# A state-space stage rebuilt: convolution folded into the projection, and the last norm of the mixture moved into it

## The reference

```python
xz = x @ W_in + b_in                       # 128 -> 512
x_main, gate = xz[..., :256], xz[..., 256:]
x_main = silu(causal_conv(x_main, conv_w, taps=3, per channel) + conv_b)
dt = sigmoid(x_main @ W_dt + b_dt); Bm = x_main @ W_B + b_B; Cm = x_main @ W_C + b_C
state = (1 - dt) * state + dt * Bm;  y = Cm * state        # a scan over the 1024 tokens
y = (y - mean(y)) * rsqrt(var(y) + 1e-5)                   # over the 64 states
y = y @ W_si + b_si + D * x_main
y = y * sigmoid(gate)
out = y @ W_out + b_out
```

## Time and profile before

| | |
|---|---|
| median of 3 runs | 829.82 us (828.91 to 830.15) |
| profiled execution | 827.14 us, span of the trace 825.4 us |
| TensorE busy | 740.8 us, 90% of the span |
| VectorE, ScalarE, GpSimd busy | 462.3, 390.0, 439.0 us |
| mean granted TensorE clock | 0.956 of full |
| first mixture, from its first load to its last addition | 501 to 637 us |
| state space, first projection to the second mixture's first matmul | 643.0 to 703.0 us |

### The profile page before, as it was taken

One profiled execution on the slowest core, in us unless ns is written; L12 is line 12 of the kernel. 1 busy time (PEld: TensorE's weight loads), 2 busy tenths in 40 slices (PEclk: granted clock), 3 DMA queues, 4 the chain that ended last, 5 costly groups with the idle time before them and its releaser, 6 DMA issues. The chain is left out here.

```text
span 825.4 us, 14251 instructions
## 1 busy us (share of the span) xinstructions
PE 740.8 (90%) x5448; PEld 495.9 (60%) x5448; DVE 462.3 (56%) x1232; ACT 390.0 (47%) x483; POOL 439.0 (53%) x316
## 2 busy tenths in 40 slices
PE   2789999999999999999999989988998856679998
PEld 2456555655555565556556547867887522657787
DVE  5765565666556556655755501555455774655343
ACT  2345556555555555555555441355444740255422
POOL 4356775676667658656855680044343553144343
PEclk9699999999999999999999999999999885899999
DMA  2000000000000000000000006132231000033232
GB/s 64 8 1 1 9 1 1 8 1 2 8 1 2 7 2 1 8 2 1 2 1 26 2 1 147 27 120 87 66 104 39 0 1 0 0 106 113 67 106 77
DMA packets 29459, 25.15 MB, mean 30 GB/s; under 512 B 10128, under 2 KB 20944, under 8 KB 29392
## 3 DMA queue, kind: packets, MB, share of 16 engines
q1 hardware_dynamic: 29392, 24.25, 10.1%
HBM read 22.92 MB, written 1.31 MB: 29 GB/s over the span
## 5 line engine op out<-in xcount | busy, mean ns | idle before, releaser
L378 POOL TENSOR_TENSOR all_x<-all_x,at_probs 128x1024 f32<-128x1024 f32 (+3 forms) x128 | 222.9, 1741 | 35.7 <-ACT at_probs L453 21.0
L453 ACT ACTIVATE at_probs<-at_ring 128x1024 f32<-128x1024 f32 x144 | 147.3, 1024 | 113.8 <-PE at_ring L625 107.3
L498 DVE CUSTOM_DVE_ANT_0 at_ring<-at_ring,at_after_query 128x128 f32<-128x128 f32 (+3 forms) x256 | 119.5, 521 | 74.1 <-PE at_ring L590 74.1
L643 PE MATMUL at_out<-at_probs,at_k_nat 128*64 128x512 f32 (+3 forms) x768 | 140.3, 494 | 1.1 <-DVE a_attn_t L521 0.9
L1079 POOL TENSOR_TENSOR m_prod<-m_gate,m_wb 128x512 f32<-128x512 f32 x64 | 81.8, 1283 | 110.6 <-ACT m_gate L936 85.5
L378 POOL TENSOR_TENSOR all_x<-at_probs 128x768 f32<-128x768 f32 (+1 forms) x32 | 66.9, 2091 | 126.5 <-ACT at_probs L453 126.3
L990 DVE TENSOR_TENSOR m_hid<-m_prod,m_u 128x512 f32<-128x512 f32 x64 | 44.0, 687 | 88.7 <-POOL m_prod L1079 84.4
L643 PEld LDWEIGHTS at_out<-at_probs,at_k_nat 128*64 128x64 f32 x768 | 49.2, 136 | 69.9 <-issue 66.0
L494 DVE TENSOR_REDUCE at_half_max<-at_ring 128x2 f32<-128x1024 f32 x64 | 75.5, 1222 | 12.4 <-PE at_ring L590 12.4
L936 ACT ACTIVATE m_gate<-m_g 128x512 f32<-128x512 f32 x72 | 42.9, 599 | 82.2 <-PE m_g L847 81.7
L855 PEld LDWEIGHTS m_acc<-rest_wd,m_hid 128*128 128x128 f32 x576 | 75.9, 194 | 6.2
(11 more groups left out here) (196 smaller groups left out, 1293.4 us busy)
## 6 DMA issues: line engine op xcount, KB each, us to landing
m_wb<-m_wt_far SPq DMA_DIRECT2D x128, 128.0 KB, 2.9
all_x<-in_L_attn_a_x SPq DMA_DIRECT2D x8, 256.0 KB, 3.7
at_w_raw<-in_L_attn_a_W_qk SPq DMA_DIRECT2D x8, 128.0 KB, 2.6
out<-all_x SPq DMA_DIRECT2D x4, 256.0 KB, 2.3
a_room<-in_L_attn_a_W_out SPq DMA_DIRECT2D x1, 512.0 KB, 4.0
m_raw_wg<-in_L_ffn_experts_wg SPq DMA_DIRECT2D x1, 512.0 KB, 4.8
m_raw_wu<-in_L_ffn_experts_wu SPq DMA_DIRECT2D x1, 512.0 KB, 4.2
rest_wd<-in_L_ffn_experts_wd SPq DMA_DIRECT2D x1, 512.0 KB, 4.2
```

What stands on the lines that cost most here:

```text
L378: return pool.tensor_tensor(sums[:, :, a * P:b * P], left, right, ALU.add)
L453: act.activation(probs[:, :, slot * BANK:(slot + 1) * BANK], pair("S", unit, slot)[:, :, :], ACT.Exp, scale=BETA).then_inc(exp_done, 1)
L498: last = dve.tensor_tensor_reduce(out=sums_ps, in0=sums_ps, in1=after_query[:, BANK - w:BANK], scale=1.0, scalar=MASKED, op0=ALU.add, op1= ...
L643: last = pe.matmul(out_ps[rows(l), o:o + (b - a) * P], k_nat[g % 3][:, j, rows(l)], probs[:, l, at:at + (b - a) * P], start=(j == 0), stop ...
```

## The change

- The projection weights are multiplied by each of the three taps ahead of time (`scale_taps`, on GpSimd in the first mixture, ahead of the fourth residual), so that the convolution is three projections added up in PSUM, of columns shifted by 0, 1 and 2. The first two columns of a sequence take one-column fp32 matmuls, and a two-row matmul takes the bias off where the padding is (`edges`). SP loads W_in in two parts, the taps as a row on all partitions (384 KB) and a bias row.
- Silu becomes a sigmoid on ScalarE and one VectorE operation on the same bank: (bank + bias) times sigmoid. `biases` makes the joined bias.
- Banks: a ring of four for main, gate and output projections, three for dt, B, C, one for turning.
- The last group's final norm of the first mixture is taken out of that mixture and stands inside the state space (`late`); main tiles 0 to 5 don't need it.
- The order on all engines is new: four main tiles, two gates, `states(0)`, then the other main tiles between the steps of the first half's chain, six gates between those of the second.
- The norm of y subtracts the mean in one operation ahead of the root, and multiplies in one, in place of eight scalings. Tables of ScalarE are loaded by name ahead of need. Six of the eight gate products are on VectorE, two on GpSimd.

```diff
@@ -725,7 +725,7 @@
-            if piece in FINISH and (with_finish or piece == "add_up"):
+            if piece in FINISH and (with_finish and n + 1 < GROUPS or piece == "add_up"):
                 found.append((FINISH[piece] + STEPS * (n + 1), piece, n, "finish"))
@@ -1081,6 +1081,8 @@
+                    if ahead_of and n + 1 == GROUPS:
+                        ahead_of.scale_taps(pool)
@@ -1136,11 +1138,14 @@
     def __init__(self, s, ins):
         KT = INNER // P
         self.ins, self.loaded, self.w_in_loaded = ins, s.sem("ssm_loaded"), s.sem("ssm_w_in_loaded")
-        self.split = s.sem("ssm_split")
-        self.w_in = s.sb("w_in", [P, 2 * INNER])
-        self.w_in_hi, self.w_in_lo = s.sb("w_in_hi", [P, 2 * INNER], F32R), s.sb("w_in_lo", [P, 2 * INNER], F32R)
+        self.scaled, self.split = s.sem("ssm_scaled"), s.sem("ssm_split")
+        self.w_main, self.tap_row = s.sb("w_main", [P, INNER]), s.sb("tap_row", [P, INNER, TAPS])
+        self.b_row, self.edge = s.sb("b_row", [2, INNER]), s.sb("edge", [2, INNER])
+        wide = [P, TAPS + 1, INNER]
+        self.w_raw, self.w_hi, self.w_lo = s.sb("w_raw", wide), s.sb("w_hi", wide, F32R), s.sb("w_lo", wide, F32R)
         self.b_in = s.sb("b_in", [P, 2 * KT])
         self.conv_w, self.conv_b, self.skip = s.sb("conv_w", [P, KT, TAPS]), s.sb("conv_b", [P, KT]), s.sb("skip", [P, KT])
+        self.bias = s.sb("bias", [P, KT])
@@ -1156,7 +1161,11 @@
-        sp.dma_start(self.w_in[:, :], ins["W_in"]).then_inc(self.w_in_loaded, 16)
+        sp.dma_start(self.w_main[:, :], ins["W_in"][:, 0:INNER]).then_inc(self.w_in_loaded, 16)
+        sp.dma_start(self.w_raw[:, TAPS, :], ins["W_in"][:, INNER:2 * INNER]).then_inc(self.w_in_loaded, 16)
+        sp.dma_start(self.tap_row[:, :, :].rearrange("p c t -> p (c t)"),
+                     ins["conv_w"].rearrange("c t -> (c t)").partition_broadcast(P)).then_inc(self.w_in_loaded, 16)
+        dma(self.b_row[:, :], ins["b_in"][0:INNER].partition_broadcast(2))
         dma(self.b_in[:, :], col(ins["b_in"]))
         dma(self.conv_w[:, :, :], ins["conv_w"].rearrange("(c p) t -> p c t", p=P))
@@ -1172,29 +1181,38 @@
+    def scale_taps(self, pool):
+        pool.wait_ge(self.w_in_loaded, 16 * 3)
+        for t in range(TAPS):
+            pool.tensor_tensor(self.w_raw[:, t, :], self.w_main[:, :], self.tap_row[:, :, t], ALU.mult)\
+                .then_inc(self.scaled, 1)
     def split_high(self, act):
-        act.wait_ge(self.w_in_loaded, 16)
-        act.activation(self.w_in_hi[:, :], self.w_in[:, :], ACT.Copy).then_inc(self.split, 1)
+        act.wait_ge(self.scaled, TAPS)
+        act.activation(self.w_hi[:, :, :], self.w_raw[:, :, :], ACT.Copy).then_inc(self.split, 1)
     def split_low(self, dve):
         dve.wait_ge(self.split, 1)
-        dve.tensor_tensor(self.w_in_lo[:, :], self.w_in[:, :], self.w_in_hi[:, :].bitcast(FP32), ALU.subtract)
+        dve.tensor_tensor(self.w_lo[:, :, :], self.w_raw[:, :, :], self.w_hi[:, :, :].bitcast(FP32), ALU.subtract)
...
+SETS = BATCH * (INNER // P)
+SSM_USES = [("main", i) for i in range(SETS)] + [("gate", 0), ("gate", 1)] + \
+    [("main", SETS + i) for i in range(SETS)] + [("out", i) for i in range(SETS)] + \
+    [("gate", i) for i in range(2, 2 * SETS)] + [("out", SETS + i) for i in range(SETS)]
+SSM_BANKS = 4
...
+        def bank(what, i):
+            return ring[number[(what, i)] % SSM_BANKS]
+        def bank_free(pe, what, i):
+            at = number[(what, i)] - SSM_BANKS
+            if at >= 0:
+                before, j = SSM_USES[at]
+                pe.wait_ge({"main": xs_done, "gate": gate_done, "out": closed}[before], j + 1)
+        def tile(i):
+            h, j = divmod(i, SETS)
+            return h, j // KT, j % KT
+        def out_tile(i):
+            h, j = divmod(i, SETS)
+            return h, j % BATCH, j // BATCH
...
+                pool.wait_ge(late.normed, 1)
+                pool.tensor_tensor(k.x[:, :, :], k.x[:, :, :], each, ALU.add)
...
+                    h, b, c = tile(i)
+                    pool.wait_ge(xs_done, i + 1)
+                    pool.tensor_scalar(z[c][:, tokens(b, h)], xs[c][:, tokens(b, h)], v.skip[:, c:c + 1],
+                                       b_si[:, c:c + 1], ALU.mult, ALU.add).then_inc(skipped, 1)
+                for i in (SETS, SETS + 2):
+                    h, b, c = out_tile(i)
+                    pool.wait_ge(closed, i + 1)
+                    pool.wait_ge(gate_done, 2 * SETS)
+                    pool.tensor_tensor(z[c][:, tokens(b, h)], z[c][:, tokens(b, h)], sg[c][:, tokens(b, h)], ALU.mult)
...
+                def main(i):
+                    h, b, c = tile(i)
+                    bank_free(pe, "main", i)
+                    out = bank("main", i)
+                    if i == 0:
+                        pe.wait_ge(edged, 2)
+                    if b * 2 + h == LATE:
+                        pe.wait_ge(late.low, 1)
+                    for t in reversed(range(TAPS)):
+                        back = TAPS - 1 - t
+                        skip = 2 if h == 0 and back else 0
+                        at = b * SEQ + h * BANK
+                        o, r = out[:, skip:BANK], slice(at + skip - back, at + BANK - back)
+                        hi, lo = [w[:, t, c * P:(c + 1) * P] for w in (v.w_hi, v.w_lo)]
+                        pe.matmul(o, hi, k.xhi[:, r], start=(back == 0), stop=False, skip_group_check=True)
+                        pe.matmul(o, hi, k.xlo[:, r], start=False, stop=False, skip_group_check=True)
+                        last = pe.matmul(o, lo, k.xhi[:, r], start=False, stop=(t == 0), skip_group_check=True)
+                    if h == 0:
+                        for part in (k.xhi, k.xlo):
+                            pe.matmul(out[:, 1:2], v.w_raw[:, 1, c * P:(c + 1) * P], part[:, b * SEQ:b * SEQ + 1].bitcast(FP32),
+                                      start=False, stop=False, skip_group_check=True)
+                        last = pe.matmul(out[:, 0:2], v.edge[:, c * P:(c + 1) * P], k.ident[0:2, 0:2], start=False, stop=True,
+                                         skip_group_check=True)
+                    last.then_inc(main_ready, 1)
...
+                def outputs(half_of):
+                    pe.wait_ge(yt_done, half_of + 1)
+                    for i in range(SETS * half_of, SETS * (half_of + 1)):
+                        h, b, c = out_tile(i)
+                        bank_free(pe, "out", i)
+                        pe.matmul(bank("out", i)[:, :], w_si[r, c * P:(c + 1) * P], yt[r, half(h)],
+                                  start=True, stop=True).then_inc(out_ready, 1)
...
+                def use_main(i):
+                    _, _, c = tile(i)
+                    act.wait_ge(main_ready, i + 1)
+                    if i == 0:
+                        act.wait_ge(summed_up, 4)
+                    wait(act, xs_done, i - 1)
+                    act.activation(sig[i % 2], bank("main", i)[:, :], ACT.Sigmoid, bias=v.bias[:, c:c + 1])\
+                       .then_inc(main_sig, 1)
...
+                    act.preload_act_table_set("sqrt_and_others")
...
+                    act.preload_act_table_set("sigmoid_and_others")
...
+                def edges():
+                    taps = v.tap_row[0:2, :, :]
+                    dve.scalar_tensor_tensor(out=v.edge[:, :], in0=taps[:, :, 1], scalar=k.ident[0:2, 0:1],
+                                             in1=taps[:, :, 0], op0=ALU.mult, op1=ALU.add).then_inc(edged, 1)
+                    dve.wait_ge(edged, 1)
+                    dve.scalar_tensor_tensor(out=v.edge[:, :], in0=v.edge[:, :], scalar=-1.0, in1=v.b_row[:, :],
+                                             op0=ALU.mult, op1=ALU.mult).then_inc(edged, 1)
+                def biases():
+                    w = v.conv_w
+                    dve.tensor_tensor(v.bias[:, :], w[:, :, 0], w[:, :, 1], ALU.add).then_inc(summed_up, 1)
+                    dve.wait_ge(summed_up, 1)
+                    dve.tensor_tensor(v.bias[:, :], v.bias[:, :], w[:, :, 2], ALU.add).then_inc(summed_up, 1)
+                    dve.wait_ge(summed_up, 2)
+                    dve.tensor_tensor(v.bias[:, :], v.bias[:, :], v.b_in[:, 0:KT], ALU.mult).then_inc(summed_up, 1)
+                    dve.wait_ge(summed_up, 3)
+                    dve.tensor_tensor(v.bias[:, :], v.bias[:, :], v.conv_b[:, :], ALU.add).then_inc(summed_up, 1)
+                    dve.wait_ge(summed_up, 4)
+                def silu(i):
+                    h, b, c = tile(i)
+                    dve.wait_ge(main_sig, i + 1)
+                    dve.scalar_tensor_tensor(out=xs[c][:, tokens(b, h)], in0=bank("main", i)[:, :], scalar=v.bias[:, c:c + 1],
+                                             in1=sig[i % 2], op0=ALU.add, op1=ALU.mult).then_inc(xs_done, 1)
...
+                    dve.wait_ge(varied, h + 1)
+                    then(dve.tensor_tensor(y_c[:, h, :, :], natural, bcast(moments[:, h, :, 0], STATE), ALU.subtract))
```

(83 more changed lines are left out.)

169 lines of the change are left out of this document (57 added, 112 removed).

## The result

The changed kernel took **816.7 us** (median of 4, 814.91 to 819.88) against 829.74 before: ratio 0.9848, 95% interval 0.9816 to 0.9881, that is 10 to 15 us less. A second series of six gave 817.49, ratio 0.9875 (0.985 to 0.9901). By its interval that is 8 to 12 us less. The forecast was 818.7, with a range from 815 to 824, and 11.1 us less.

The account below looks back on a forecast made before the run. The state space was taken as bound by a chain of small hand-overs between two barriers. 12.5 us saved there, less 1.1 for the clock and 0.3 outside, gave 11.1 us and 818.7 us, range 815 to 824.

Parts of the forecast that it names:

- the prediction's own signs of being wrong: Half clock beyond the stage's first 4 us, or the first mixture's last addition later than 638.
- The stage is a chain between barriers: State space: small hand-overs between two block barriers, nothing beside them to hide a shortening; 53.1 us instead of 65.6.
- the 1.1 charged for the clock: State space's tail: TensorE stands still twice and may drop to half clock, lengthening the last outputs by 1.1 us.
- Small fp32 matmuls, 0.115 a record: First-half projection tiles: three small fp32 matmuls each, 0.115 us a record, bounds 0.05 and 0.3; tile 2.75 us.
- Rival (b): Dearer front: small fp32 matmuls at 0.3 us a record, walk 4.4 later, 821.5 to 826 us; chance 0.20.
- First matmul after `edges`, 2.0: Stage's front: TensorE waits for statistics and two edge operations of 0.35 us each; first matmul 2.0 to 2.5 after start.
- Half clock of 3.5 us in the front, +1.7: Stage's front: TensorE, coming out of idle, runs 3.5 us at half clock as before, adding 1.7 us.
- First half's chain and filling: Middle of the stage: remaining main tiles fill TensorE between first-half steps; `states(0)` at 654.4, `states(1)` at 671.7.
- Tail, 12.35 to the barrier's end: From second y at 678.1 through turn, norm, outputs and additions to the barrier at 690.45.
- rival (c): ScalarE table changes dearer, each 1.28 us more: walk 3.4 us later, 822.1 us; chance 0.07.
- Rival (e): TensorE's granted clock stays at half level throughout the stage: 848.6 us; chance 0.04.
- First mixture, 0.3 with up to 1.5 for the port: GpSimd's three tap products fit its 2.10 us wait; if dearer or holding VectorE's norm, up to 1.5; 0.3 taken.

Follow-up runs that it names:

- late_start: Changed kernel with tap products spread, edge and bias operations moved into the first mixture, and TensorE waiting for the late norm: 816.86 us, ratio 0.9865.
- edges_early: Changed kernel with the six small edge and bias operations moved out of the state space into the first mixture: 815.24 us, ratio 0.9861.
- norm_back: Changed kernel with the last norm put back behind the first mixture's end, which also let GpSimd add `b_out` at the barrier: 826.56 us, ratio 0.9974.
- gates_first: Changed kernel with all eight gate projections and sigmoids ahead of `states(0)`: 824.39 us, ratio 0.9946 to the kernel before.
- m1_part_alone: Kernel before with only the change's first-mixture work (loads, tap products, wider splits), results unread: 828.36 us, ratio 1.0019.
- taps_spread: Changed kernel with the three tap products placed one each behind the weightings of steps 14, 15 and 16: 816.05 us, ratio 0.9872.
- warm_start: Changed kernel with eight unread transposes of the identity on TensorE ahead of the first main tile: 816.87 us, ratio 0.9859.
- before_bias_later: Kernel before with GpSimd's `b_out` addition moved behind the eight skip terms: 826.04 us, ratio 0.9977.

## Why the prediction held

The total and the sign were right; the measured gain, 10 to 15 us by the interval, holds the 11.1. The mechanism was right too, a chain between two barriers whose tail is shortened by doing the first half's end ahead of it: the forecast's second y ends at 678.1 where the old one ended at 678.95, so nearly all of its gain lies behind that y, and it does. That the total came so close is partly luck, for two errors on the clock were of nearly the same size. And both of the prediction's own signs of being wrong appeared. The half clock lasted until 10.1 us behind the barrier, beyond the first 4, which was the mis-sized term below. The last addition came at 640.44, later than 638; but that was no sound sign, for in the second profile of before it came at 639.65. Step by step:

- **The stage is a chain between barriers.** Right. It measured 55.6 us from the end of the last addition to the next mixture. Forecast were 53.4 by the walk and 54.5 with the 1.1 charged for the clock.
- **Small fp32 matmuls, 0.115 a record.** Right: 0.12 at the full clock. Rival (b) falls. A whole tile took 2.9 instead of 2.75.
- **First matmul after `edges`, 2.0.** 2.24: the two operations took 0.51 and 0.41 instead of 0.35 each. That this wait costs more than its length was not in the forecast.
- **Half clock of 3.5 us in the front, +1.7.** The mis-sized term: it was 6.7 us in both profiles of the changed kernel, +3.3, and 3.1 in another run with the same stage. With 0.2 of edges it is nearly the whole excess of the front. The 3.5 was a misreading of the kernel before. Its window began at 643, and the clock had fallen 3.3 us ahead of that, while the norm ran, as windows of TensorE in that trace show:

```profile
639.70:643.00 3.30, 1.09 (x4) 0.51 0.00 0
643.00:646.60 3.60, 3.58 (x9) 0.50 0.00 0
```

So the half clock lasted 6.9 us there too, and half of it fell on a stretch with four transposes. With the norm gone from that place, what there is of it meets the projections. late_start and edges_early show where it comes from: TensorE's standing still between the mixture's last down projection and tile 0. It was 3.25 us in the changed kernel. How long it lasts stays open: counted from the fall it was 6.8 us at this place in eight of the fourteen profiles, 3.4 in three, 13.7 in norm_back and nothing in the two with 1.05 us of standing still.
- **First half's chain and filling.** From `states(0)` to `states(1)` 17.6 us, forecast 17.3. Right. No `silu` alone took more than 0.75 us, as expected.
- **Tail, 12.35 to the barrier's end.** 12.0. Right; but the 1.1 charged for a falling clock did not come: with the gates between it stayed at 0.97, and at 0.63 in gates_first without them. So the two errors on the clock nearly cancelled: 1.6 too little in front, 1.1 too much behind.
- **Gates as filling.** 5.9 us by gates_first: 4.1 of work out of the way, and 1.4 in the tail, where the clock fell.
- **The two operations at 685.93 and 686.87.** The prediction has the second within the first. They overlap for 0.33 us only; that the second took its usual 0.69 all the same still agrees with it.
- **Table loads.** Loads and roots follow each other with no drain in the profile after, as in the earlier trace rows; rival (c) falls:

```profile
670.47 0.30 ACT L1415 ACTIVATE ss_sd<-ss_moments,all_eps 128x8 f32<-128x8 f32 x1 [0.31 <-DVE ss_moments L89]
670.79 1.28 ACT L1416 ACT_TABLE_LOAD   x1
672.09 1.37 ACT L1398 ACTIVATE a_attn_t<-ss_ring,rest_bias 128x512 f32<-128x512 f32 x2
```

- **Rival (e)**, the half clock throughout, falls too: behind its front the stage has 1.00 and 0.97.
- **First mixture, 0.3 with up to 1.5 for the port.** About the upper bound came: 1.6 by m1_part_alone (interval 0 to 3.1), and 1.6 between the means of the profiles, whose ranges overlap. The products took 2.30 us beside a gap of 2.10; what reached the end was VectorE's norm, 0.9 us longer beside them. I had named that and took 0.3 of it.

What stays open: what sets the length of the half clock, and how the gain outside the norm's place (4 us) divides between the new order, the convolution in TensorE and the freed `b_out` stall. That the new order made the tail short is read from the two timelines, and no run has the old order with the rest changed; moving `b_out` alone gave 1.9 before the change, and no run has the convolution alone. The single figures don't add up, since each edit alone meets the next wait.

## What to carry to other kernels

When the chain's first engine stands still across a barrier, look at what it waits for first: two operations on a tile of two partitions (0.9 us), behind the late norm's statistics (1.2), held TensorE 2.2 us, and with the clock that cost 5.3 us of the stage, or 3.7 where the half clock was short (taps_spread). Read the clock from where it fell, and not from where your window begins. Price an engine's large instruction by whom it locks out, not by its own queue; moved from one gap to another, it finds the next victim. In a chain of two halves, what only the first half needs goes ahead of the second half's last link. Filling belongs where the chain is thin: the same six gates cost 5.9 us ahead of it.

## What the runs showed of the hardware

- The fall of TensorE's clock came after it had stood still, in the changed kernel not at once: at 643.65 it began at 2.4 GHz and was at 1.2 from 644.7, in the midst of dense matmuls, for 6.7 us. In taps_spread, after the same 3.26 us of standing still, it was at 1.2 GHz when the first tile began, and for 3.1 us. In the kernel before it fell while TensorE stood still. The Trainium skill (TensorE: Matmul & The Clock Gate, HAM oscillation) tells of such falls after idle stretches; the runs agree in that 1.05 us of standing still left the clock at 1.00 and 3.2 to 4.1 us brought it to 0.50. Eight transposes (1.06 us) in such a gap did not prevent the fall (warm_start).
- A GpSimd instruction reading SBUF held even a VectorE operation on 2 partitions for its whole length: 4.81 us instead of 0.51. It also stretched operations with one operand in SBUF: 2.25 us instead of 1.11 for four scalings, and 2.07 instead of 0.41 for `ss_decay` in before_bias_later. The Trainium skill (SBUF — State Buffer, Who interferes with whom) counts a `tensor_scalar` among the operations that can take the shared ports; the trace agrees that they are held, and the prediction, which names both halves of the rule, took 0.3 us for the norm.
- The skip terms, unchanged on GpSimd, took 0.77 us instead of 1.25, now that VectorE's work beside them reads PSUM and one SBUF operand instead of two. before_bias_later bears this out in one kernel: four of them beside the convolution steps took 6.42 us, and the four behind those steps 3.03. The group of the changed kernel's instructions by line:

```profile
L1282 POOL TENSOR_SCALAR m2w_z<-a_attn_t,rest_skip,rest_b_si 128x512 f32<-128x512 f32 x8 | 6.1, 769 | 21.4 <-DVE a_attn_t L1483 21.4
```
